# A two-layer kernel in one program: a late feed-forward part moved between two LayerNorms, and five instruction lists placed anew

## What is computed

```python
h = layernorm(x) * (1 + ca) + sa;  x = x + ga * L0_attn(h)   # gated delta rule, 16 heads of 8
h = layernorm(x) * (1 + cb) + sb;  x = x + gb * L0_ffn(h)    # 8 experts 128->512->128, top 2
h = layernorm(x) * (1 + ca) + sa;  x = x + ga * L1_attn(h)   # conv, decays, normalized scan
h = layernorm(x) * (1 + cb) + sb;  x = x + gb * L1_ffn(h)    # 128->512, gelu, 512->128
```

## Time and profile before

| | before |
|---|---|
| median of three runs | 498.4 us |
| the profiled execution | 498.22 us |
| its span, first to last instruction | 496.4 us |
| TensorE busy | 429.8 us (87%) |
| ScalarE busy | 369.8 us (74%) |
| VectorE busy | 340.4 us (69%) |
| GpSimd busy | 170.0 us (34%) |
| ScalarE table loads | 69 (39 at L1419, 30 at L1417), 1283 ns each |
| last product of the last expert's first matrix (`first(5, 7, 3)`) ends | 451.9 us |

### The profile page before, as it was taken

How to read it: one execution, slowest core, us unless ns; L and a number is a source line. 1 busy time by engine, 2 the same in 40 slices (tenths; PEclk the granted TensorE clock), 3 DMA queues, 4 the chain that set the end, 5 groups by cost and what they waited for, 6 DMA issues and landing times.

```text
span 496.4 us, 7099 instructions
## 1 busy us (share of the span) xinstructions
PE 429.8 (87%) x2152; PEld 311.5 (63%) x2152; DVE 340.4 (69%) x851; ACT 369.8 (74%) x663; POOL 170.0 (34%) x233
## 2 busy tenths in 40 slices
PE   5597797869998798999989999999999878999266
PEld 2395674646776576667667665777676656797034
DVE  2335977975799973999999998987434671223941
ACT  5979779996977759699649875757997789546434
POOL 1060763484267871267940260163100002000000
PEclk9869989998999899999999999999999999999869
DMA  7838795006800128400058200000001000000000
GB/s 191 287 104 220 230 364 128 3 8 170 216 15 1 29 58 210 114 0 1 2 135 207 68 1 22 0 2 1 1 0 23 0 1 1 22 0 2 0 0 21
DMA packets 34340, 35.46 MB, mean 71 GB/s; under 512 B 12792, under 2 KB 30336, under 8 KB 34048
## 3 DMA queue, kind: packets, MB, share of 16 engines
q1 hardware_dynamic: 34016, 30.84, 23.6%
q10 hardware_dynamic: 288, 4.19, 2.2%
HBM read 13.78 MB, written 1.05 MB: 30 GB/s over the span
## 4 chain that ended last, share of the span: by engine, by line
PE 56%; ACT 14%; DVE 13%; issue 7%; SPq 3%; POOL 3%; DMA 2%; DVEq 0%; POOLq 0%; ACTq 0%
PE psF L844 16%; PE psS L859 15%; PE psB L800 3%; SPq L601 3%; PE psM L907 2%; PE psM L899 2%; DMA wrep<-XX 2%; PE psM L677 2%; ACT L1417 2%; ACT L1419 2%; DVE zb L2146 2%; ACT hid L1613 2%; DVE XX L2182 1%; PE psB L687 1%; DVE norm L2173 1%
## 5 line engine op out<-in xcount | busy, mean ns | idle before, releaser
L859 PEld LDWEIGHTS psS<-we2s,hid 128*128 128x128 f32 x1024 | 129.7, 193 | 33.1 <-issue 27.1
L844 PE MATMUL psF<-h,we1s 128*128 128x256 f32 (+1 forms) x384 | 136.5, 465 | 8.0 <-ACT hid L1613 6.0
L1613 ACT ACTIVATE hid<-psF,col 128x256 f32<-128x256 f32 (+1 forms) x192 | 99.7, 542 | 53.2 <-PE psF L844 49.7
L859 PE MATMUL psS<-we2s,hid 128*128 128x128 f32 x1024 | 131.3, 276 | 5.8 <-DVE acc L2231 5.7
L844 PEld LDWEIGHTS psF<-h,we1s 128*128 128x128 f32 x384 | 66.6, 195 | 39.0 <-issue 17.5
L3249 POOL TENSOR_TENSOR QS<-H,qn 128x256 f32<-128x256 f32 x64 | 57.7, 909 | 86.9 <-DVE H L2217 84.2
L2231 DVE SCALAR_TENSOR_TENSOR acc<-psS,gate,acc 128x128 f32<-128x128 f32 x128 | 41.5, 342 | 46.4 <-PE psS L859 46.3
L2217 DVE TENSOR_TENSOR_SCAN H<-A,psT 128x320 f32<-128x320 f32 x64 | 52.2, 816 | 1.3
L1419 ACT ACT_TABLE_LOAD x39 | 50.0, 1283 | 1.4 <-PEq L3544 0.7
L2196 DVE TENSOR_TENSOR psT<-wrep,H 128x360 f32<-128x360 f32 x64 | 40.0, 626 | 13.8 <-DMA wrep<-XX 12.1
L3283 POOL TENSOR_TENSOR x<-x,gdb 128x512 f32<-128x512 f32 (+1 forms) x5 | 4.4, 871 | 131.7 <-PE psM L677 131.5
(11 more groups left out here) (254 smaller groups left out, 659.1 us busy)
## 6 DMA issues: line engine op xcount, KB each, us to landing
wrep<-XX SPq DMA_DIRECT2D x72, 160.0 KB, 3.3
krep<-kn SPq DMA_DIRECT2D x64, 128.0 KB, 2.5
hid<-fold_mats_dram SPq DMA_DIRECT2D x22, 256.0 KB, 3.7
we1s<-we_dram ACTq DMA_DIRECT2D x1, 2048.0 KB, 9.0
we2s<-we_dram ACTq DMA_DIRECT2D x1, 2048.0 KB, 15.7
outT_dram<-x SPq DMA_DIRECT2D x3, 256.0 KB, 3.7
M<-mats_dram SPq DMA_DIRECT2D x1, 576.0 KB, 5.4
x<-xT_dram SPq DMA_DIRECT2D x2, 256.0 KB, 7.1
```

Source lines behind the costliest of these rows:

```text
L844: mm(bank[name][:, 0:(b - a) * TWS[w]], we1s[:, e, k * P:(k + 1) * P], h2[w % 2][:, a * TWS[w]:b * TWS[w]], start=True, stop=True).then_in ...
L859: last = mm(bank[name][:, t * P:(t + 1) * P], hid[n % 2][:, k, t * P:(t + 1) * P], we2s[:, e, k, :], start=(k == 0), stop=(k == HT - 1))
L1613: nc.scalar.activation(hid[x_ % 2][:, k, 0:c], psF[n % 2][:, 0:c], ACT.Silu, bias=pc("be1", HT * e + k)).then_inc(s_hid_done, 1)
```

## The change

`ln_order()` takes the LayerNorm of the feed-forward part of unit 2 out of its place and puts it behind that of the attention part of unit 3. The lists are written anew to go with it. No operation is added or taken away but products of constants: before there are seven calls of `fill`, four over layer 0 (32, 23, 35, 37) and three in the tail (2, 25, 34); after it there are eight, one near the start (38), one among the experts of unit 4 (44), 48 and 67 among the last experts, and four in the tail (35, 62, 45, 54).

```diff
             order.append(("moe", r + 1))
         if v:
             order.append(("ffn", v[0]))
-    order += [("ssd", LASTS[0]), ("ssd", LASTS[1]), ("ffn", LASTS[0]), ("ffn", LASTS[1])]
+    late = ("ffn", LASTS[0] - 1)
+    order.remove(late)
+    order += [("ssd", LASTS[0]), late, ("ssd", LASTS[1]), ("ffn", LASTS[0]), ("ffn", LASTS[1])]
     return {key: i for i, key in enumerate(order)}
```

TensorE's list, from the last experts of unit 4 on:

```diff
             second(4, 3, 1)
-            for i in range(1, 4):
+            fill(44)
+            for i in range(0, 3):
                 first(4, 5, i)
             second(4, 4, 0)
+            first(4, 5, 3)
             second(4, 4, 1)
+            first(4, 6, 0)
             ssd_out(2)
-            for i in range(0, 3):
-                first(4, 6, i)
-            center(("ffn", 2))
+            first(4, 6, 1)
+            first(4, 6, 2)
+            second(4, 5, 0)
             first(4, 6, 3)
-            second(4, 5, 0)
-            variance(("ffn", 2))
+            first(4, 7, 0)
             second(4, 5, 1)
-            for i in range(0, 3):
-                first(4, 7, i)
+            first(4, 7, 1)
             second(4, 6, 0)
+            first(4, 7, 2)
             first(4, 7, 3)
             second(4, 6, 1)
-            ffn_up(2, 0)
+            first(5, 0, 0)
+            first(5, 0, 1)
             second(4, 7, 0)
-            first(5, 0, 0)
-            for i in range(1, 4):
-                ffn_up(2, i)
-            first(5, 0, 1)
-            ffn_down(2)
             first(5, 0, 2)
             first(5, 0, 3)
             second(4, 7, 1)
...
             second(5, 4, 1)
+            second(5, 5, 0)
             first(5, 6, 0)
             first(5, 6, 1)
-            second(5, 5, 0)
+            center(("ssd", 3))
             first(5, 6, 2)
             first(5, 6, 3)
             second(5, 5, 1)
-            first(5, 7, 0)
-            first(5, 7, 1)
+            for i in range(0, 4):
+                first(5, 7, i)
             variance(("ssd", 3))
-            first(5, 7, 2)
-            first(5, 7, 3)
+            fill(48)
+            center(("ffn", 2))
             second(5, 6, 0)
+            variance(("ffn", 2))
             second(5, 6, 1)
             second(5, 7, 0)
+            fill(67)
             second(5, 7, 1)
             experts_back(5)
+            for i in range(0, 4):
+                ffn_up(2, i)
+            ffn_down(2)
             ssd_steps(3)
+            ssd_in(3)
             center(("ssd", 4))
-            ssd_in(3)
+            fill(35)
             variance(("ssd", 4))
-            fill(2)
+            fill(62)
             ssd_steps(4)
             ssd_in(4)
             ssd_out(3)
@@ -1390,11 +1389,11 @@
             center(("ffn", 3))
             center(("ffn", 4))
             variance(("ffn", 3))
-            fill(25)
+            fill(45)
             variance(("ffn", 4))
             ffn_up(3, 0)
             ffn_up(3, 1)
-            fill(34)
+            fill(54)
             ffn_up(3, 2)
             ffn_up(3, 3)
             ffn_up(4, 0)
```

ScalarE's list:

```diff
-            ln_square(("ffn", 2))
-            hidden(4, 6, 3)
-            ln_scale(("ffn", 2))
-            hidden(4, 7, 0)
-            hidden(4, 7, 1)
-            modulate(("ffn", 2))
-            hidden(4, 7, 2)
-            hidden(4, 7, 3)
             for i in range(0, 4):
-                ffn_act(2, i)
+                hidden(4, 7, i)
             for i in range(0, 4):
                 hidden(5, 0, i)
             for i in range(0, 4):
...
                 hidden(5, 7, i)
             ln_scale(("ssd", 3))
+            ln_square(("ffn", 2))
             modulate(("ssd", 3))
+            ln_scale(("ffn", 2))
+            modulate(("ffn", 2))
+            for i in range(0, 4):
+                ffn_act(2, i)
             ssd_steps(3)
+            ssd_in(3)
             ln_square(("ssd", 4))
-            ssd_in(3)
             ln_scale(("ssd", 4))
             modulate(("ssd", 4))
             ssd_steps(4)
-            ssd_decay(3)
             ssd_in(4)
             ssd_gate(3)
+            ssd_decay(3)
+            ssd_shifted(3)
             ssd_decay(4)
-            ssd_shifted(3)
             ssd_gate(4)
             ssd_shifted(4)
```

VectorE's list (`ssd_halo(4)` was after `mix(5, 3, 0)`):

```diff
             mix(4, 5, 0)
+            ssd_halo(3)
             mix(4, 5, 1)
-            ln(("ffn", 2))
             mix(4, 6, 0)
             mix(4, 6, 1)
             mix(4, 7, 0)
-            ffn_residual(2)
+            ssd_residual(2)
             mix(4, 7, 1)
             mix(5, 0, 0)
+            experts_residual(4)
             mix(5, 0, 1)
             mix(5, 1, 0)
             mix(5, 1, 1)
-            experts_residual(4)
-            ssd_halo(3)
...
             mix(5, 5, 1)
+            ln(("ssd", 3))
             mix(5, 6, 0)
+            ln(("ffn", 2))
             mix(5, 6, 1)
-            ln(("ssd", 3))
             mix(5, 7, 0)
             mix(5, 7, 1)
+            ffn_residual(2)
             experts_residual(5)
+            ssd_halo(4)
             ssd_sum(3)
             ssd_tap(3, 0)
             ssd_least(3)
+            ln(("ssd", 4))
             ssd_tap(3, 1)
-            ln(("ssd", 4))
             clear_last()
```

```diff
             ffn_act(0, 0)
+            ffn_act(0, 1)
+            hidden(3, 1, 2)
+            ffn_act(0, 2)
+            ffn_act(0, 3)
+            hidden(3, 1, 3)
+            gate_rows(3)
+            hidden(3, 2, 0)
+            hidden(3, 2, 1)
             router_bias(3)
-            for i in range(1, 4):
-                ffn_act(0, i)
-            hidden(3, 1, 2)
```

More of the change, by code:

```diff
@@ L918, in _ @@
             first_modulation()
-            fill(32)
+            fill(38)
             center(("front", 1))
-            for i in range(0, 4):
+            for i in range(0, 5):
                 project(0, i)
             variance(("front", 1))
-            project(0, 4)
             square_sums(0, 0)
@@ L1113, in _ @@
             second(2, 0, 2)
+            second(2, 0, 3)
+            project(4, 4)
+            experts_back(1)
             first(2, 2, 0)
[L1115 to L1116 removed]
             gate_rows(2)
@@ L1358, in _ @@
             first(5, 5, 0)
-            center(("ssd", 3))
             first(5, 5, 1)
@@ L2484, in _ @@
             solve_rest(0, 2)
-            for i in range(0, 3):
-                tap(1, 1, i)
+            tap(1, 1, 0)
+            carry_hf(2)
+            ln(("front", 2))
+            tap(1, 1, 1)
+            tap(1, 1, 2)
             for i in range(0, 3):
@@ L2673, in _ @@
             chunk_outer(2, 8)
+            mix(1, 0, 0)
             chunk_scan(2, 8)
             chunk_seed(2, 9)
+            experts_residual(0)
             chunk_delta(2, 9)
@@ L2767, in _ @@
+            route_top(2)
+            up_bias()
             chunk_seed(3, 4)
             chunk_delta(3, 4)
+            route_sum(2)
+            tap(4, 2, 0)
+            chunk_outer(3, 4)
+            tap(4, 2, 1)
+            chunk_scan(3, 4)
+            route_inverse(2)
+            mix(1, 7, 0)
+            chunk_seed(3, 5)
+            mix(1, 7, 1)
+            tap(4, 2, 2)
             route_gate(2)
+            chunk_delta(3, 5)
+            tap(4, 3, 0)
+            experts_residual(1)
@@ L2789, in _ @@
             chunk_scan(3, 7)
-            mix(2, 0, 3)
-            ln(("ssd", 0))
+            for i in range(0, 4):
+                mix(2, 0, i)
             chunk_seed(3, 8)
@@ L3021, in _ @@
             route_sum(4)
-            mix(3, 6, 2)
-            mix(3, 6, 3)
-            mix(3, 7, 0)
+            mix(3, 7, 1)
+            mix(3, 7, 2)
             route_inverse(4)
-            for i in range(1, 4):
-                mix(3, 7, i)
             route_gate(4)
+            mix(3, 7, 3)
             ffn_residual(1)
```

1076 lines of the change are left out of this document (522 added, 554 removed).

## The result

Measured beside each other, the kernel before took 498.09 us (median of 4 runs, 496.78 to 500.36) and the changed kernel 507.48 us (4 runs, 506.18 to 509.46). The ratio is 1.0187 with a 95% interval of 1.0137 to 1.0237: slower, and whether by more or less than 2% is open. The profiled execution of the changed kernel took 506.18 us.

A forecast was written before the change was run, and what follows sets the result against it. TensorE, with 56% of the chain of waits, was taken as the main bound, but idle in the tail. Terms -11.7 + 16.1 + 0 = +4.4 us on the profiled 498.2 us gave 502.6 us, range 496.5 to 508.

The forecast's parts named there:

- Rival 3: Between 280 and 375 us, added table loads fall on TensorE's path, about half of 7.7 us: 506.5 us; chance 0.13.
- Rival 4: In the tail, new gaps lower TensorE's clock, doubling ups and ffn_down on the chain, up to 4 us: 506.6 us; chance 0.07.
- The experts' stretch shortens by 11.7 us: From 404.6 us to the end of first(5, 7, 3), work and waits leave: 11.7 us, bounds 8.6 and 12.3.
- TensorE stands for `ln(("ssd", 3))`, `center(("ffn", 2))` at +3.2 us: In the tail, center waits for bank X1, which ln frees: TensorE stands from about +1.3 to +3.2 us.
- `ssd_sum(4)` 16.1 us later, and from there nothing changes: The tail costs 16.1 us up to ssd_sum(4), bounds 10.0 and 20; behind it everything runs as before.
- T: The moment first(5, 7, 3) ends, forecast at 440.2 us against 451.9 before; times in the tail count from it.
- Order on VectorE is part of it: In the tail, experts_residual(5) sits behind ffn_residual(2), though its input was ready 9 us before, and holds center(("ssd", 4)).
- If T is off 440 by more than 2 us, it was the lists over layer 0: A sign: first(5, 7, 3) ending over 2 us from 440 would point to layer 0's lists, rivals 2 and 3.
- rival 2: The new lists over layer 0 gain about what the tail loses, 3.6 us or more: 499 us; chance 0.17.
- Rival 1: In the tail, the moved part overlaps and ScalarE's work alone decides: cost 10.0 us, time 496.5 us; chance 0.13.
- The table load without a second price: In the tail, loads cost 1.28 us each without the skill's drain of about 1380 ns, which would add 2.7 us.
- The ends are -6.2 and +7.7; I take 0, the middle: Lists over layer 0: gains from waits and three fewer fills against six more table loads, taken as 0 us.

The follow-up runs named there:

- e1: Kernel before with its lists up to the middle of expert unit 4, the changed lists and LayerNorm order behind it: 504.25 us, ratio 1.0133.
- e7: e1 with one more product of constants, fill(49), in the 2.06 us idle ahead of center(("ffn", 2)): 503.80 us, ratio 1.0090.
- e12: Changed kernel with ffn_down(2) writing bank B and ffn_residual(2) behind experts_residual(5) and ssd_halo(4) on VectorE: 505.13 us, ratio 1.0157.
- e4: Before's lists to mid expert unit 4; unit 2's feed-forward LayerNorm behind unit 4's attention LayerNorm, its work spread over free banks: 493.24 us, ratio 0.9912.
- e8: e4 with eight products of constants in TensorE's idle time ahead of ffn_up(2, 0): 490.86 us, ratio 0.9832.
- e10: Changed kernel with before's lists up to about 245 us, new ones from there on, changed tail: 504.33 us, ratio 1.0147.
- e2: Changed lists up to the middle of expert unit 4, lists and LayerNorm order of the kernel before from there on: 500.8 us, ratio 1.0059.
- e6: Kernel before without its fills 23, 35 and 37 over layer 0: 499.38 us, ratio 0.9996.
- e3: Changed kernel with two edits of VectorE's list taken back, the places of ln(("moe", 0)) and of window 0's first eight routing calls: 506.51 us, ratio 1.0175.
- e9: Changed kernel with new lists only up to about 245 us, before's from there to the middle of expert unit 4, changed tail: 514.68 us, ratio 1.0344.
- e5: Changed kernel with three products of constants put back over layer 0: 508.66 us, ratio 1.0204.
- e11: Changed kernel with VectorE's and GpSimd's lists of before up to the middle of expert unit 4: 541.23 us, ratio 1.0873.

## Why the prediction was right, and where it was off

The direction held, and so did the mechanism in the tail, nearly link by link. The number is in part luck: 507.48 us is outside the forecast's own 500.5 to 505, and lies 0.5 us inside the range only because the range reached up for rivals 3 and 4, neither of which shows in the profile. The forecast's 502.6 us is 4.9 us too low. By the profiles 3.4 us of that are explained (the spans differ by 7.8 us where the sum gave 4.4: 4.3 more from the lists over layer 0, 0.3 and 0.65 less from the two other terms). The other 1.5 us is mainly the difference between the medians and the profiled executions; the falls of the clock seen in e1 and e7 are of that size, but that they make it is not shown.

- *The experts' stretch shortens by 11.7 us.* It did by 12.0, in every kernel that has the new order there.
- *TensorE stands for `ln(("ssd", 3))`, `center(("ffn", 2))` at +3.2 us.* It started at +3.35 behind 2.06 us of idle. `ffn_down(2)` was done at +18.9 (forecast +18.6), `ffn_residual(2)` at +20.55 (+20.4), `experts_residual(5)` at +21.3 (+21.3), `center(("ssd", 4))` at +21.4 (21.3).
- *`ssd_sum(4)` 16.1 us later, and from there nothing changes.* It starts 27.95 us after T instead of 11.88: 16.07. From T to the end it was 15.45; the 0.6 us was won behind `ssd_out(3)`.
- *Order on VectorE is part of it.* e12 shows the wait.
- *If T is off 440 by more than 2 us, it was the lists over layer 0.* T is 444.25, and it was they, but neither by the gain of rival 2 nor by the table loads of rival 3.
- *Rival 1 (ScalarE's work alone decides)* is out for this order. With its 10.0 us it gave 496.5; e4 and e8 show that it was pessimistic for another place of the same work.
- *Rival 3 (table loads on TensorE's path)* came near in time, 506.5 us, and is wrong in its cause: e10, and TensorE busy 80.0 of 80 us in the window from 280 to 360.
- *Rival 4 (the clock)* didn't happen in the changed kernel's profile. In three of the eight profiled executions with this stall it did, for 1.4 to 1.6 us, not up to 4.
- *The table load without a second price.* At 455.43 the GELU table loads for 1.28 us and the next GELU starts at 456.73, 0.02 us behind it: again only the first of the two numbers that the Trainium skill (ScalarE: Activation LUTs, What ACT_TABLE_LOAD costs) gives.

**The term that was mis-sized** is "The ends are -6.2 and +7.7; I take 0, the middle" (the middle is in fact +0.75). The lists over layer 0 cost 4.3 us in the profiles, and 0.6% alone (e2). Both ends were wrong: the three fills, 2.6 us of the gain, gave nothing when taken out (e6), and the table loads, the whole of the loss, cost 0.1%, inside the intervals (e10). I had set what goes against the loads that come, and had not asked for waits that the new order adds. One stands beside the very place that I counted as a gain. The timeline of the changed kernel, for the earlier trace rows:

```profile
167.57 1.10 PE L734 MATMUL psM<-norm,C 128*128 128x512 f32 x2 [1.72 <-DVE hf L2086]
171.15 3.76 PE L861 MATMUL psS<-we2s,hid 128*128 128x128 f32 x16 [2.48 <-DVE acc L2221]
```

The wait for a `mix`, 2.13 us before, is 2.48 now: the two quarters of an expert are ahead of it, used up while nothing was missing. And the wait of 1.44 us for `experts_residual(0)` is gone for one of 1.72 for a LayerNorm. What followed is in the windows of before, and then of the changed kernel:

```profile
76.00:96.00 20.00, 14.38 (x61) 9.38 (x59) 16.71 (x40) 18.49 (x33) 7.65 (x9) 0.91 0.31 75
...
156.00:184.00 28.00, 23.77 (x109) 18.17 (x108) 25.63 (x55) 19.36 (x34) 22.56 (x27) 0.94 0.16 39
```

```profile
76.00:96.00 20.00, 14.32 (x52) 10.24 (x52) 14.06 (x37) 16.60 (x30) 3.03 (x5) 0.74 0.31 74
...
156.00:184.00 28.00, 22.60 (x106) 17.29 (x105) 26.11 (x58) 19.49 (x35) 22.41 (x30) 0.88 0.15 39
```

From 76 to 96 us TensorE is as busy as before, but for nine instructions less: at a clock of 0.74, 14.32 us hold what 10.6 would at full speed, against 13.1 before. Summed over twelve such windows up to 404 us, TensorE idles 1.2 us more (45.1 against 43.9) and loses 3.3 us more to the lower clock (busy time by one less the granted clock, 13.9 against 10.5), 4.5 together, near the 4.3. This is an estimate, and its split is loose: the same two sums are 52.4 to 53.5 us in all for e1, e7, e8 and e10, whose lists there are before's in whole or up to 245 us, against 54.4 in the kernel before, and 57.3 to 59.0 for e2, e3, e12 and the changed kernel with the new lists.

That is where the time went, not yet why. The clock alone doesn't explain it: e8, with before's lists, also had 0.74 from 76 to 96 us and `ssd_out(2)` at 405.15, while e2, with the new lists, had 0.91 there and `ssd_out(2)` at 407.08. e10 puts the loss ahead of 245 us, but only as a remainder, since e9, the direct test, is spoiled by its own seam. Which calls do it stays open; giving back the two waits that I suspected didn't help (e3).

## What to carry to other kernels

When work is moved out of a stretch that one engine fills, the gain is easy to price; the bill comes where the work lands, and there the chain has to be followed through every engine's list, with the call that happens to stand behind the moved one (`experts_residual(5)`). The same work a few calls later, beside a chain that leaves two engines idle, turned 1.0133 (e1) into 0.9912 (e4), and with eight products of constants into 0.9832 (e8), all with before's lists over layer 0. And a large rewrite of matched lists isn't zero because its edits seem to balance: look for new waits at each place where a call was brought forward, as well as for old ones that go.

## What the runs showed of the hardware

- Behind one and the same idle time of 2.06 us TensorE's granted clock stayed at 1.00 in five executions and fell in three, to 0.51 over 3 us in e1 (about 1.2 of 2.4 GHz). A product of 512 columns then took 2.04 us instead of 1.10 there. Behind 1.25 us of idle at `ssd_steps(4)` it fell in e7, e9 and e10 (0.50 to 0.57 over 2.5 us) and not in the changed kernel, e1, e3, e5, e11 and e12. Of these, e9 and e10 have exactly the changed kernel's tail. So the same list in the tail meets one clock or the other.
- Behind 7.69 us of idle the clock was 0.50 for 6 us (e4); with products of constants over all but 0.82 us of it, 1.00 (e8). That was worth 2.6 us from T to the end, for work that nothing reads.
